# A two-layer decoder block: norms centred by a matmul, gate products as factors of the exponentials, feed-forward scales taken earlier

## What is computed

```python
x = x + rwkv(layernorm(x))                      # 16 heads x 64, exponentials, running sums, sigmoid
x = x + cross_attention(layernorm(x), ctx, ctx, boxes)
x = x + ffn(layernorm(x))                       # 4-bit block weights, 16-bit activations, maxima over the whole tensor
x = x + self_attention(layernorm(x))
x = x + cross_attention_2(layernorm(x), ctx, ctx)
x = x + int8_matmul(layernorm(x))
# layernorm: (x - mean(x)) / sqrt(var(x) + 1e-5)
# the box gate of the first cross-attention:
g  = relu(einsum('bnmd,hd->bhnm', emb, Wg) + bg)   # emb: sines and cosines of logs of box distances
mn = softmax(log(clip(g, 1e-6)) + q @ k.T / 8)
# feed-forward weights: 4 bits in blocks of 32
s  = max(|w| over 32) / 7;  w = clip(round(w / s), -8, 7) * s
```

## Time and profile before

| | |
|---|---|
| median of 3 runs | 364.59 us (364.56 to 365.57) |
| the profiled execution | 364.24 us, of which the span is 362.5 us |
| PE busy | 305.4 us (84%) |
| DVE busy | 282.2 us (78%) |
| ACT busy | 214.8 us (59%) |
| POOL busy | 83.7 us (23%) |
| chain that ended last | PE 55%, DVE 21%, ACT 13%, issue 6% |

### The profile page before, as it was taken

The page is one execution under the profiler, slowest core; times in us unless marked ns, Lnnn a source line. Parts: engine busy times, 40 slices in busy tenths (PEclk is TensorE's granted clock), DMA queues, the critical chain, the costliest instruction groups (busy, mean ns, idle before and its releaser), DMA issues.

```text
span 362.5 us, 8272 instructions
## 1 busy us (share of the span) xinstructions
PE 305.4 (84%) x3406; PEld 178.5 (49%) x3406; DVE 282.2 (78%) x425; ACT 214.8 (59%) x363; POOL 83.7 (23%) x81
## 2 busy tenths in 40 slices
PE   5186989887899989999999898957779899999882
PEld 1032323222333467778877675422224577777761
DVE  2979999888899649879986845698842778998776
ACT  2939786868998534655457465578742445565431
POOL 4001656454667000001900000000001524222000
PEclk9776999999999999999999999995596999999997
DMA  5595000003567591000000000000000022210001
GB/s 168 192 276 239 1 1 0 2 0 66 90 147 158 99 294 77 5 0 4 2 2 2 2 4 0 3 0 0 0 0 0 2 40 33 36 21 4 4 2 58
DMA packets 31492, 18.41 MB, mean 51 GB/s; under 512 B 26464, under 2 KB 28768, under 8 KB 30816
## 3 DMA queue, kind: packets, MB, share of 16 engines
q1 hardware_dynamic: 31456, 17.89, 18.9%
HBM read 11.59 MB, written 5.24 MB: 46 GB/s over the span
## 4 chain that ended last, share of the span: by engine, by line
PE 55%; DVE 21%; ACT 13%; issue 6%; DMA 1%; SPq 1%; POOL 1%; DVEq 0%; ACTq 0%; POOLq 0%
PE psum L475 50%; PE psum L862 3%; PE psum L669 2%; ACT arena_b L1257 2%; ACT arena_a L1103 2%; ACT arena_b L1075 1%; ACT arena_b L1095 1%; DVE arena_a L1620 1%; ACT arena_a L1064 1%; DVE arena_a L1605 1%; DVE small L1610 1%; DVE arena_a L1612 1%; DVE small L1618 1%; ACT arena_b L1210 1%; DVE arena_b L1761 1%
## 5 line engine op out<-in xcount | busy, mean ns | idle before, releaser
L1360 POOL TENSOR_TENSOR arena_a<-arena_a,arena_b 128x1024 f32<-128x1024 f32 x15 | 31.8, 2120 | 45.9 <-DVE arena_b L1509 45.9
L475 PE MATMUL psum<-arena_b 64*64 64x9 f32 (+2 forms) x804 | 38.3, 289 | 1.9 <-ACT arena_b L1230 0.8
L1521 DVE TENSOR_TENSOR_SCAN arena_a<-arena_b,psum 128x512 f32<-128x512 f32 x32 | 37.3, 1205 | 0.3
L1803 DVE TENSOR_REDUCE small<-psum 128x16 f32<-128x1024 f32 x16 | 19.6, 1224 | 13.0 <-PE psum L475 12.5
L475 PEld LDWEIGHTS psum<-arena_b 64*64 64x64 f32 (+2 forms) x804 | 19.3, 138 | 17.9 <-issue 16.4
L475 PE MATMUL psum<-xc,logg 128*128 128x512 f32 x32 | 20.2, 718 | 8.3 <-DVE sq L1495 7.7
L1257 ACT ACTIVATE arena_b<-psum 128x512 f32<-128x512 f32 x32 | 17.5, 595 | 15.4 <-PE psum L862 15.4
L475 PE MATMUL psum<-arena_a 64*64 64x64 f32 (+1 forms) x576 | 25.2, 265 | 0.5 <-DVE arena_a L1640 0.5
L475 PEld LDWEIGHTS psum<-arena_a 64*64 64x64 f32 (+1 forms) x576 | 13.7, 140 | 15.8 <-issue 13.6
L475 PE MATMUL psum<-xw,const 128*128 128x512 f32 x24 | 17.8, 857 | 3.4 <-DVE small L1714 3.4
L1516 DVE SCALAR_TENSOR_TENSOR arena_b<-psum,par,arena_b 128x1024 f32<-128x1024 f32 x16 | 20.4, 1276 | 0.2
(11 more groups left out here) (238 smaller groups left out, 703.1 us busy)
## 6 DMA issues: line engine op xcount, KB each, us to landing
g_scratch<-arena_a SPq DMA_DIRECT2D x64, 64.0 KB, 2.6
logg<-g_scratch SPq DMA_DIRECT2D x4, 1024.0 KB, 6.1
logg<-in_rkvo SPq DMA_DIRECT2D x8, 256.0 KB, 4.4
xw<-in_xw SPq DMA_DIRECT2D x1, 2048.0 KB, 8.6
logg<-arena_a SPq DMA_DIRECT2D x8, 128.0 KB, 2.4
ffn_w<-in_ffn SPq DMA_DIRECT2D x1, 576.0 KB, 9.5
x<-in_xT SPq DMA_DIRECT2D x2, 256.0 KB, 3.5
arena_a<-in_ctxT SPq DMA_DIRECT2D x1, 512.0 KB, 4.3
```

The costliest lines, as they stand in the source:

```text
L475: return nc.tensor.matmul(o, l, r, start=start, stop=stop, **kw)
L1360: g.tensor_tensor(two, two, pairs[n % 3][:, :, HALF + 1:], ALU.add).then_inc(s.ab_done, 1)
L1521: return v_.tensor_tensor_scan(sums[n % 3][:, i * HALF:(i + 1) * HALF], pairs[n % 3][:, i, 0:HALF], scan_mask, 0.0, ALU.add, ALU.mult)
L1803: v_.tensor_reduce(mx.rearrange("p (r h) -> p r h", r=4), s4, axis=AX.X, op=ALU.max).then_inc(s.a_max, 1)
```

## The change

Four things are done at once. (1) For norms 0 to 3 TensorE multiplies x by `centre`, which VectorE now makes at the very start; the centred value stays in PSUM, ScalarE squares it there and VectorE scales it from there, so that `ln_centre` on VectorE is gone; banks and the order of the instructions around move to make room. (2) ScalarE's `box_relu(k)` is run in step k+2, in front of `r_e`, and not at the end of step k+1. (3) The logarithms are gone: the maximum is taken of the scores alone, the exponential gets the factor 0.125, and `x_gated`, two new instructions a tile on VectorE, multiplies by g + 1e-6 behind it. `s_scaled` is now given by the difference. (4) `block_scales` runs ahead of the first scores. Besides, the box angles are reduced before they are moved by DMA, and the counts of `keep_running` change around the feed-forward stage.

```diff
+        def centre_bank(n, h):
+
+            return half(pC if n == 3 and h else pA, 1 if n == 3 else h)
+
         def var_bank(n, h):
-
-            if n == 2:
-                return half(pC if h else pA, h)
-            return half(pC if n == 4 else pB, h)
+            return half(pC if n == 2 and h else pB, 1 if n == 2 else h)
...
             def box_moved(k, t):
 
+                sp.wait_ge(s.box_cl, 2 - k)
                 for h in range(2):
...
                         r = 32 * (2 * bh + h)
                         sp.dma_start(box_half(angle, h)[64 * bh + 32 * k:64 * bh + 32 * k + 32], t[r:r + 32])\
                             .then_inc(s.box_in[h], 16)
 
-            sp.wait_ge(s.box_wh, 1)
             box_moved(1, box_wh)
-            sp.wait_ge(s.box_mv, 1)
             box_moved(0, box_xy)
...
             def store_g(bh, i):
 
                 k = 2 * bh + i
-                sp.wait_ge(s.g_log, 4 * i + 2 * bh + 2)
+                sp.wait_ge(s.g_relu_act if bh else s.g_relu_dve, 4 * i + 4)
...
-            def ln_mean(n, h):
-                mm(half(pA, h), mean_w, half(x, h)).then_inc(s.ln_mean, 1)
+            def ln_centre(n, h):
+                mm(centre_bank(n, h), centre, half(x, h)).then_inc(s.ln_xc, 1)
...
-            pe.wait_ge(s.const_in, 16)
+            pe.wait_ge(s.centre_set, 1)
             for h in range(2):
                 pe.wait_ge(s.x_in[h], 16)
-                ln_mean(0, h)
+                ln_centre(0, h)
...
             def x_q(j):
 
                 if j == 0:
-                    pe.wait_ge(s.ln_xc, 4)
                     pe.wait_ge(s.ln_done, 3)
-                elif j >= 2:
+                elif j == 1:
+                    pe.wait_ge(s.ln_ln, 4)
+                else:
                     pe.wait_ge(s.s_scaled, j - 1)
                 if j == 4:
                     pe.wait_ge(s.ln_done, 4)
                 for i in range(4):
                     cc = 4 * (j % 2) + i
-                    last = mm((pD if j == 1 else pA)[:, 256 * i:256 * i + 256], wq[:, cc * P:(cc + 1) * P],
+                    last = mm((pD if j == 0 else pB if j == 1 else pA)[:, 256 * i:256 * i + 256], wq[:, cc * P:(cc + 1) * P],
                               xn[:, 256 * (j // 2):256 * (j // 2) + 256])
...
@@ -649,6 +648,8 @@
                 pe.wait_ge(s.kx_done, t // 2 * 2 + 2)
                 if t >= 1:
                     pe.wait_ge(s.s_scaled, t)
+                else:
+                    pe.wait_ge(s.ln_done, 4)
...
             x_q(0)
+            ln_var(1, 1)
             x_k(1)
             x_q(1)
-            ln_var(1, 1)
             x_scores(0)
...
+            nc.tensor.transpose(pB[:, 0:P], l1w[:, 7 * P:8 * P], ident).then_inc(s.r_t, 1)
             def context_keys(h):
 
                 pe.wait_ge(s.l1_in, 16)
-                if h:
-                    pe.wait_ge(s.w_done, 1)
-                mm(half(pC if h else pB, 0), l1w[:, 4 * P:5 * P], half(ctx_all, h)).then_inc(s.kv_psum, 1)
+                mm(half(pC, 0) if h else half(pD, 1), l1w[:, 4 * P:5 * P], half(ctx_all, h)).then_inc(s.kv_psum, 1)
...
-            context_keys(0)
             x_wo(TILES - 1)
-            pe.wait_ge(s.r_q, 1)
-            nc.tensor.transpose(pD[:, 512:576].bitcast(BF16), r8T[:], ident16[:]).then_inc(s.r_qs, 1)
-            pe.wait_ge(s.r_dg, 1)
-            mm(pD[:, 640:768], mean_w, r_diag).then_inc(s.r_row_p, 1)
             pe.wait_ge(s.x2_done, TILES)
             pe.wait_ge(s.w_done, 1)
-            ln_mean(2, 1)
+            ln_centre(2, 1)
+            pe.wait_ge(s.r_q, 1)
+            nc.tensor.transpose(pB[:, P:P + 64].bitcast(BF16), r8T[:], ident16[:]).then_inc(s.r_qs, 1)
+            pe.wait_ge(s.r_dg, 1)
+            mm(pB[:, 2 * P:3 * P], mean_w, r_diag).then_inc(s.r_row_p, 1)
+            ln_var(2, 1)
+            context_keys(0)
             context_keys(1)
-            ln_var(2, 1)
+            pe.wait_ge(s.r_row_s, 1)
             context_values()
...
-            keep_running(1)
+            pe.wait_ge(s.kv_done, 1)
             spread_max(0)
             keep_running(2)
             pe.wait_ge(s.kv_done, 3)
-            pe.wait_ge(s.ln_xc, 6)
-            pe.wait_ge(s.ln_ln, 6)
+            pe.wait_ge(s.ln_done, 6)
...
+            keep_running(2)
             spread_max(2)
+            keep_running(2)
             pe.wait_ge(s.f_rec, 3)
             keep_running(1)
             spread_max(3)
+            keep_running(1)
             pe.wait_ge(s.f_rec, 4)
+            keep_running(5)
+            spread_max(4)
             keep_running(2)
-            spread_max(4)
-            keep_running(1)
...
                         pe.wait_ge(s.x3_done, 1)
-                        ln_mean(3, 0)
+                        ln_centre(3, 0)
...
             ln_var(3, 0)
             pe.wait_ge(s.x3_done, 2)
-            ln_mean(3, 1)
+            ln_centre(3, 1)
             ln_var(3, 1)
-            pe.wait_ge(s.ln_done, 7)
+            keep_running(1)
...
             pe.wait_ge(s.ln_ln, 8)
             project(0)
-            keep_running(2)
-            pe.wait_ge(s.ln_xc, 8)
+            keep_running(1)
+            pe.wait_ge(s.ln_done, 8)
             scores(0)
             project(1)
...
             def ln_square(n, h):
                 act.wait_ge(s.ln_xc, 2 * n + h + 1)
-                nc.scalar.activation(half(sq, h), half(xc, h), ACT.Square).then_inc(s.ln_sq, 1)
+                nc.scalar.activation(half(sq, h), centre_bank(n, h), ACT.Square).then_inc(s.ln_sq, 1)
...
-                    act.wait_ge(s.box_cl, h + 1)
+                    act.wait_ge(s.box_in[h], 4 * 16)
                     nc.scalar.activation(box_half(folded, h), box_half(angle, h), ACT.Abs).then_inc(s.box_fold, 1)
...
-            def log_g(k):
-                cc, bh, i = k % 2, k // 2 % 2, k // 4
-                act.wait_ge(s.g_relu_act if bh else s.g_relu_dve, 4 * i + 3 + cc)
-                at = (8 * cc + 4 * bh + 2 * i) * HALF
-                nc.scalar.activation(g_sb[:, at:at + 2 * HALF], g_sb[:, at:at + 2 * HALF], ACT.Ln, bias=der[:, 28:29])\
-                    .then_inc(s.g_log, 1)
...
                 if n + 2 < RWKV_STEPS:
                     r_eu(n + 2)
                 r_er(n)
+                if 2 <= n <= GATES + 1:
+                    box_relu(n - 2)
                 if n + 2 < RWKV_STEPS:
                     r_e(n + 2)
                 r_er1(n)
-                if n <= GATES:
-                    box_relu(n - 1)
-                if LOG_STEPS <= n < LOG_STEPS + 8:
-                    log_g(n - LOG_STEPS)
...
             def x_queries(j):
+                source = pA if j else pD
                 act.wait_ge(s.q_psum, j + 1)
                 for i in range(4):
                     cc = 4 * (j % 2) + i
-                    last = nc.scalar.activation(q_x[j // 2 % 2][:, cc, :], pA[:, 256 * i:256 * i + 256], ACT.Identity,
+                    last = nc.scalar.activation(q_x[j // 2 % 2][:, cc, :], source[:, 256 * i:256 * i + 256], ACT.Identity,
                                                 bias=p("xbq", cc))
...
             def x_exponentials(t):
-                act.wait_ge(s.s_sub, t + 1)
-                nc.scalar.activation(s_x[t % 2], s_x[t % 2], ACT.Exp).then_inc(s.s_exp, 1)
+                act.wait_ge(s.s_scaled, t + 1)
+                nc.scalar.activation(s_x[t % 2], s_x[t % 2], ACT.Exp, scale=0.125).then_inc(s.s_exp, 1)
...
+                nc.scalar.activation(half(k1_ctx, h), half(pC, 0) if h else half(pD, 1), ACT.Copy).then_inc(s.kv_done, 1)
+
+            ln_square(2, 1)
+            ln_rstd(2, 1)
             keys_kept(0)
-            ln_square(2, 1)
             keys_kept(1)
-            ln_rstd(2, 1)
...
-            g.tensor_tensor(centre, ident, mean_w, ALU.subtract).then_inc(s.a_ones, 1)
...
             def ln_scale(n, h):
                 dve.wait_ge(s.ln_rstd, 2 * n + h + 1)
-                o, a, b = half(xn, h), half(xc, h), half(sq, h)
+                o, a, b = half(xn, h), centre_bank(n, h), half(sq, h)
...
+            dve.wait_ge(s.const_in, 16)
+            v_.tensor_tensor(centre, ident, mean_w, ALU.subtract).then_inc(s.centre_set, 1)
             dve.wait_ge(s.consts_set, 2)
-            dve.wait_ge(s.x_in[0], 16)
-            ln_centre(0, 0)
-            dve.wait_ge(s.x_in[1], 16)
-            ln_centre(0, 1)
...
-            for h in range(2):
-                f, k = box_half(angle, h), box_half(turns, h)
-                dve.wait_ge(s.box_in[h], 4 * 16)
+            for f, k, ready in ((box_wh, box_half(turns, 0), s.box_wh), (box_xy, box_half(turns, 1), s.box_mv)):
+                dve.wait_ge(ready, 1)
...
             r_y(n)
-            dve.wait_ge(s.x1_done, 1)
-            ln_centre(1, 0)
             residual1(1)
...
             def x_centred(t):
 
                 if t == 0:
+                    for k in range(2):
+                        dve.wait_ge(s.g_out[k], 16 * 16)
+                sx, mx = s_x[t % 2], small[:, 80:96]
```

(59 more changed lines are left out.)

35 lines of the change are left out of this document (11 added, 24 removed).

## The result

The changed kernel took 355.41 us (median of four runs, 353.99 to 359.60) beside 364.57 for the kernel before: ratio 0.973, 95% interval 0.968 to 0.978. The ratio leaves out the run of 359.60, which had a lower granted clock (0.957) than the other three (0.968 to 0.972). Its profiled execution took 354.20 (span 352.4), where the sum of the prediction said 354.0; for the median it said 354.3.

| stretch, by landmarks of the two timelines | forecast | measured |
|---|---|---|
| start, to the second divisor | -0.4 | -0.41 |
| gate steps and the steps after them, to the last residual of the stage | -6.9 | -8.23 |
| into the scores, to the first transposes | +1.0 | +2.52 |
| tiles 0 to 5 | -0.2 | -0.01 |
| tiles 6 and 7 | +3.0 | +2.67 |

A forecast was written before the change was run, and what follows sets the result against it. No single bound: a ring of waits in the gate steps, TensorE in cross-attention, reductions and low clock in feed-forward. -0.4 - 6.9 + 1.0 - 0.2 + 2.0 - 5.75 = -10.25 from 364.24: 354.0, median 354.3; range 351.8 to 360.0.

The forecast's parts named there:

- Gate steps: RWKV stage: relu a step later cuts the ring of waits; seven steps 37.5 us instead of 44.43, -6.9.
- VectorE's 5.36: Gate steps: VectorE, the fullest engine once the ring of waits is cut, sets 5.36 us a step.
- Rival B: Gate steps: another ring, say through `r_decay`; only the logarithms' removal gains, -3.1 instead of -6.9, 358.1 us; chance 0.14.
- Into the scores: Up to the first transposes: work moved ahead starts the scores 1.5 us later; +1.0, ends 0 and +2.
- 0.6 goes: From first scores to first transposes: of 9.74 us, 0.6 goes, the second half's scale having moved ahead.
- rival D: Both ends of the cross-attention: the moves there cost 3.5 us more than reckoned, 357.8 us; chance 0.13.
- Tiles 6 and 7, norm 2: End of cross-attention: +1.5 in each tile, norm 2 gives back 1.0; sum +2.0, ends +1 and +3.2.
- Feed-forward stage: Through to the second layer: held clock, shorter norm 3 and faster entry, -5.75; ends -6.5 and +2.
- the entry: Second layer's entry: one unread matmul instead of two in `project(0)`, and faster scores; gains 3.2, not the whole 3.6.
- Rival A: Feed-forward: clock falls anyway, five unread matmuls end some 4 us late; -5.75 becomes about 0, 360.0 us; chance 0.17.
- C: Low clock from feed-forward reductions until the second layer; slower than before, +3.5, 368.1 us; chance 0.04.
- Start: To the second divisor: VectorE earlier, sines no earlier; -0.4, between -1.3 (lead kept whole) and +0.5 (sines late).

The follow-up runs named there:

- the relu alone: Kernel before, with only ScalarE's relu of the gate product one step later, the eight logarithms kept: 355.59 us, ratio 0.978.
- the wait filled: Changed kernel plus two unread matmuls of 512 columns in TensorE's wait ahead of the first scores: 354.15 us, ratio 0.975.
- the kernel of 348.88: Kernel before with the relu moved, the new counts of unread matmuls, and norms 2 and 3 in the change's form: 348.88 us, ratio 0.960.
- the experiment with the angles: Kernel before with relu moved, new unread matmul counts, norms 2 and 3 changed, plus angles reduced before their moves by DMA: 348.99 us, ratio 0.957.

## Why the prediction was right, and where it wasn't

- **Gate steps.** Right in mechanism, small in size. A step takes 5.27 us, which is TensorE's busy time and now VectorE's too (28.96 of 29.00): from its relu to its scans 0.66, from there to the clip 2.23, then 0.59, 0.60 and 1.19 make 5.27. The term that failed is VectorE's 5.36. Its parts as listed add to 5.34 only, the scans overlap the next instruction by 0.09 and not 0.04 when nobody waits, and the clip takes 0.02 less. 7 x 0.09 = 0.63 of the missing 1.3; the remaining 0.7 lies in the step ahead of these (0.37) and in the steps behind, now 4.745 apart in place of 4.81, which the text had said would stay. Rival B fell with the relu alone: seven steps of 5.27 with the logarithms in.
- **Into the scores.** This is the term that was off by most, +2.52 where the forecast ended at +2. The scores start 1.29 us later counted from the last residual, the forecast 1.5. What failed is the step behind it, "0.6 goes": instead 9.74 us became 10.97. The prediction costed the scale moved ahead at its duration, and not at what the idle time that it makes does to TensorE's clock, 1.38 us in the next eight matmuls and 0.25 in the scores themselves. With the wait filled the stretch takes 21.51, +0.90 beside the 20.61 of before: but for the clock the +1.0 was right. It is rival D's place, at less than its price: the two ends of the cross-attention cost 1.0 more than reckoned (2.52 + 2.67 - 1.21 against +3.0), not 3.5.
- **Tiles 6 and 7, norm 2.** Forecast +2.0, measured +1.46. The text said rightly that `x_values` stands ahead of the exponential, and took it as given, though moving it behind gives 2.50 of the 2.67 us back.
- **Feed-forward stage.** Forecast -5.75, measured -5.49: the two spreads give 0.61 (0.6), 0.09 of it lost again between others, norm 3's second logarithm comes 1.77 earlier beyond them (1.95), the entry gives 3.20 (3.2). Rival A's clock came true from 244 to 248 alone, and its price did not: the prediction had the five unread matmuls end some 4 us late, and from VectorE's reading of the fourth spread (244.27) to the reduction that gives the fifth its maximum (250.50) lie 6.23 us, as in the kernel of 348.88 at full clock (6.24). C, slower than before, did not show.
- **Start.** -0.41 against -0.4, but the experiment with the angles says that this is chance: VectorE's lead is lost in a wait of TensorE for the sines. It is 3.30 us in the changed kernel's trace too, with a clock of 0.59 behind it (36 to 40 us). In the eight traces of kernels with this part the second divisor lay three times at 43.2 to 43.8 and five times at 45.0 to 45.2, in the six without, at 43.5 to 43.7. The sines start at 32.6 to 34.1 us in those six, at 33.1 to 33.7 in the three and at 34.1 to 35.0 in the five. The prediction said rightly that they start no earlier; the step that failed is to keep a part of VectorE's lead all the same. The range had only +0.5 on that side.
- **The total** fitted since the gate steps brought 1.3 more than reckoned, and the scores cost 1.5 more: that these two cancel is luck. Its largest term had the right cause: the relu's experiment shows it alone.
